# A third pass over edges whose messages are formed per step, and attribute sums moved to the second pass

## The reference, cut to what matters

```python
# L1: h = (relu(norm(x)) * deg_out ** -0.5) @ weight
rst = segment_sum(h[src], dst)
x = x + rst * deg_in ** -0.5 + bias
# L2: h = relu(norm(x))
msg = relu(h[src] + edge_attr)
agg = segment_sum(msg, dst)
x = x + relu((h + agg) @ W1 + b1) @ W2 + b2
# L3 norms [h[src], edge_attr] @ W1a over all edges, so it needs, beside others,
# segment_sum(edge_attr, dst) and edge_attr.T @ edge_attr
```

## Time and profile before

| | |
|---|---|
| median of 3 runs | 9793.06 us (9776.86 to 9793.11) |
| profiled execution | 9777.78 us, span 9775.0 us |
| busy: PE / PE weight load / DVE / ACT / POOL | 71% / 54% / 58% / 21% / 70% |
| second pass | 2966 to 5057 us |
| third pass | 5111 to 7280 us |
| granted TensorE clock in both | 0.50 of full speed (1.2 GHz) |

### The profile page before, as it was taken

The page is one execution under the profiler, slowest core; times in us unless marked ns, Lnnn a source line. Parts: engine busy times, 40 slices in busy tenths (PEclk is TensorE's granted clock), DMA queues, the critical chain, the costliest instruction groups (busy, mean ns, idle before and its releaser), DMA issues. The chain is left out here.

```text
span 9775.0 us, 180433 instructions
## 1 busy us (share of the span) xinstructions
PE 6948.1 (71%) x25668; PEld 5298.0 (54%) x25669; DVE 5675.3 (58%) x22992; ACT 2073.4 (21%) x8123; POOL 6813.4 (70%) x7038
## 2 busy tenths in 40 slices
PE   2666766675767888888845555555566888888886
PEld 1555555554556666666633333433445666666664
DVE  8777777776994444444455555555554444444444
ACT  5344444443120000000002222222211222222222
POOL 0677777776756777777757777777745777777773
PEclk8555555555555555555555555555555555555556
DMA  7333333333862222222212222222212333333334
GB/s 109 95 105 105 105 105 106 105 108 102 267 197 61 57 53 55 55 55 55 56 42 53 53 55 53 53 53 53 53 23 73 82 80 82 80 82 80 82 80 34
DMA packets 430593, 783.04 MB, mean 80 GB/s; under 512 B 179769, under 2 KB 208089, under 8 KB 429406
## 3 DMA queue, kind: packets, MB, share of 16 engines
q1 hardware_dynamic: 199054, 487.65, 17.4%
q0 software_dynamic: 216064, 278.76, 12.9%
q10 hardware_dynamic: 14544, 8.74, 0.5%
HBM read 634.79 MB, written 139.85 MB: 79 GB/s over the span
## 5 line engine op out<-in xcount | busy, mean ns | idle before, releaser
L1287 POOL DMA_INDIRECT arena<-node_table,idx x3328 | 3156.0, 948 | 1091.9 <-issue 813.1
L1225 PE MATMUL banks<-arena,onehot 128*128 x7040 | 2484.6, 472 | 1250.1 <-DVE onehot L1165 614.9
L1225 PEld LDWEIGHTS banks<-arena,onehot 128*128 128x128 f32 x7040 | 1758.8, 312 | 1871.4 <-issue 1659.9
L1408 POOL DMA_INDIRECT arena<-node_table,arena x1760 | 1660.6, 944 | 551.7 <-issue 381.8
L977 POOL DMA_INDIRECT sorted_edges<-arena,idx x1664 | 1611.2, 968 | 616.6 <-issue 576.1
L1165 DVE TENSOR_SCALAR onehot<-iota_row,block_base,edge_tables 128x128 f32<-128x128 f32 x3520 | 1255.6, 359 | 594.3 <-ACTq L1271 342.9
L922 PE MATMUL banks<-arena,onehot 128*128 x3520 | 1102.2, 424 | 568.0 <-DVE onehot L871 554.9
L922 PEld LDWEIGHTS banks<-arena,onehot 128*128 128x128 f32 x3520 | 882.5, 313 | 787.5 <-issue 780.8
L1173 DVE TENSOR_TENSOR arena<-arena,banks 128x65 f32 (+1 forms) x3520 | 895.2, 254 | 592.9 <-PE banks L1225 549.1
L1384 PE MATMUL banks<-arena 128*128 128x64 f32 x3520 | 1214.1, 448 | 0.0
L1379 PE MATMUL banks<-arena 128*64 128x65 f32 x3520 | 842.9, 343 | 392.1 <-ACT arena L1395 387.9
(11 more groups left out here) (291 smaller groups left out, 6152.7 us busy)
## 6 DMA issues: line engine op xcount, KB each, us to landing
arena<-sorted_edges SPq DMA_DIRECT2D x440, 524.0 KB, 4.5
arena<-in_attr_t SPq DMA_DIRECT2D x208, 512.0 KB
arena<-row_keys SPq DMA_DIRECT2D x110, 512.0 KB
arena<-in_attr_pairs SPq DMA_DIRECT2D x104, 512.0 KB
arena<-node_table,idx POOLq DMA_INDIRECT x3328, 2.5
arena<-node_table,arena POOLq DMA_INDIRECT x1760
sorted_edges<-arena,idx POOLq DMA_INDIRECT x1664, 2.3
sorted_edges<-blank_record SPq DMA_DIRECT2D x1, 6484.5 KB, 51.5
```

What stands on the lines that cost most here:

```text
L1225: nc.tensor.matmul(to, m.onehot[:, j % 4, :], rows, start=True, stop=True).then_inc(s["summed"], 1)
L1287: nc.gpsimd.indirect_dma_start(slot(j), None, m.table, bass.IndirectOffsetOnAxis(ap=m.idx[:, j:j + 1], axis=0)).then_inc(gathered[j % 32], 16)
L1408: nc.gpsimd.indirect_dma_start(slots[:, j % SLOTS, 0:D], None, m.table, bass.IndirectOffsetOnAxis(ap=rec_i[:, j % SLOTS, REC_DST:REC], axis=0)
```

## The change

Both passes keep their tiles, rings and plan. In the second pass SP loads the attributes into the same slots as the rows (`WIDE` = 129 columns: rows, attributes, one), so that one product and one add of 129 columns sum rows, attributes and the count; the gram leaves this pass. A tile counts as landed when its attributes are there too. In the third pass the in-place sum of tile j at step j goes. DVE forms the message of each step (all 1760) from the slots of its own tile into `m.messages`, a ring of eight, ACT applies ReLU there, and PE multiplies by 64 columns. DVE waits per group of eight steps for the tile of the last one. SP counts landed tiles between its loads. The gram is made in this pass, one product ahead of each of the 1664 steps. The pair rows are 130 apart (`STEP`) instead of 128.

```diff
+WIDE = 2 * D + 1
+STEP = 2 * RW
-EXT = 3644
+EXT = 3772
-    m.pair = m.both[:, 0:NB * 2 * D].rearrange("p (b f) -> p b f", b=NB)
+    m.pair = m.both[:, 0:NB * STEP].rearrange("p (b f) -> p b f", b=NB)
...
-    m.second_ring = arena[:, BOTH:BOTH + RING * RW]
-    m.gram_ring = [m.work[:, i * CH * D:(i + 1) * CH * D] for i in range(2)]
+    m.second_ring = arena[:, BOTH:BOTH + RING * WIDE]
+    assert RING * WIDE <= EXT + 2 * NODE
+    m.messages = tables[:, 1, 0:8 * D].rearrange("p (s f) -> p s f", f=D)
...
@@ -1088,77 +1091,89 @@
 def gather_by_tile(nc, m, a, layer):
     with ExitStack() as ctx:
-        s = sems(nc, "blank", "onehot", "summed", "added", "sum", "message", "landed", "grammed", "gram_done")
+        s = sems(nc, "blank", "onehot", "summed", "added", "sum", "message", "landed", "gram_done")
...
-        attr_in = ring(nc, "attr_in", CHUNKS if layer == 2 else 2)
+        attr_in = ring(nc, "attr_in", CHUNKS)
...
+        both_kinds = m.second_ring.rearrange("p (s f) -> p s f", f=WIDE)
+        rows, attrs = m.third_ring[:, 0, :], m.third_ring[:, 1, :]
+        width = {1: WIDE, 2: D}[layer]
         def slot(j):
-            return slots[:, j % RING * stride:j % RING * stride + D]
+            j = j % RING
+            return both_kinds[:, j, 0:D] if layer == 1 else rows[:, j * D:(j + 1) * D]
+        def load(sp, i, c):
+            t = i * RING + c * CH
+            sp.wait_ge(s["summed"], t + CH + NB - RING + SLACK)
+            settle(sp)
+            sp.dma_start(m.idx[:, c * CH:(c + 1) * CH], index[:, bass.ds(t, CH)]).then_inc(idx_in[c], 16)
+            to = both_kinds[:, c * CH:(c + 1) * CH, D:2 * D] if layer == 1 else \
+                attrs[:, c * CH * D:(c + 1) * CH * D].rearrange("p (s f) -> p s f", f=D)
+            frm = a["attr_t"][:, bass.ds(i * (RING * D) + c * (CH * D), CH * D)].rearrange("p (s f) -> p s f", f=D)
+            sp.dma_start(to, frm).then_inc(attr_in[c], 16)
+        def count(engine, i, j):
+            i, j = i + j // RING, j % RING
+            if j % CH == 0:
+                engine.wait_ge(attr_in[j // CH], i * 16 + 16)
+                if layer == 2:
+                    settle(engine)
+            engine.wait_ge(gathered[j % 32], i * (RING // 32 * 16) + j // 32 * 16 + 16)
+            if layer == 2:
+                settle(engine)
+            engine.sem_inc(s["landed"], 1)
         @block.sync
         def _(sp):
...
+            if layer == 1:
+                with sp.Fori(0, ROUNDS) as i:
+                    for c in range(CHUNKS):
+                        load(sp, i, c)
+            else:
+                def rounds(i, last):
+                    for c in range(CHUNKS):
+                        if c + 1 < CHUNKS:
+                            load(sp, i, c + 1)
+                        elif not last:
+                            load(sp, i + 1, 0)
+                        for j in range(c * CH + 8, min(c * CH + CH + 8, RING) if last else c * CH + CH + 8):
+                            count(sp, i, j)
+                sp.sem_inc(s["landed"], EARLY)
+                load(sp, 0, 0)
+                for j in range(8):
+                    count(sp, 0, j)
+                with sp.Fori(0, ROUNDS - 1) as i:
+                    rounds(i, False)
+                rounds(ROUNDS - 1, True)
         @block.vector
...
+            v.memset(m.both[:, NB * STEP:SPARE * STEP], 0.0).then_inc(s["blank"], 1)
             if layer == 1:
...
-            v.sem_inc(s["sum"], 2 * CH)
+                v.memset(both_kinds[:, :, 2 * D:WIDE], 1.0).then_inc(s["blank"], 1)
+                v.memset(m.pair[:, :, 0:D], 0.0).then_inc(s["blank"], 1)
...
-            def add_attr(i, j):
-                c = j // CH
-                dve.wait_ge(gathered[j % 32], i * (RING // 32 * 16) + j // 32 * 16 + 16)
-                if j % CH == 0:
-                    dve.wait_ge(attr_in[c], i * 16 + 16)
-                v.tensor_tensor(slot(j), slot(j), m.third_ring[:, 1, j * D:(j + 1) * D], ALU.add).then_inc(s["sum"], 1)
+            def add_attr(base, j, slots):
+                k = base + j
+                dve.wait_ge(s["summed"], ahead(k - 8, SLACK))
+                v.tensor_tensor(m.messages[:, j % 8, :], rows[:, bass.ds(slots[j] * D, D)], attrs[:, bass.ds(slots[j] * D, D)],
+                                ALU.add).then_inc(s["sum"], 1)
             def match(base, j, tiles, blocks):
                 dve.wait_ge(s["summed"], base + j - 3 + SLACK)
...
-                rows = m.both[:, bass.ds(blocks[j] * (2 * D), width)]
+                rows = m.both[:, bass.ds(blocks[j] * STEP, width)]
                 v.tensor_tensor(rows, rows, m.psum[j % 4][:, 0:width], ALU.add).then_inc(s["added"], 1)
-            def beats(base, units, i):
-                tiles, blocks = [], []
+            def beats(base, units):
+                tiles, blocks, slots = [], [], []
                 for j in range(units + 2):
                     if j < units:
                         if j % 8 == 0:
-                            if layer == 1:
-                                last = bounded_values(nc, ENG.DVE, plan[32:33, bass.ds(base + j + 7, 1)], TP - 1)[0]
+                            last = bounded_values(nc, ENG.DVE, plan[32:33, bass.ds(base + j + 7, 1)], TP - 1)[0]
                             blocks += group(nc, ENG.DVE, plan, 0, base + j, SPARE - 1)
                             tiles += group(nc, ENG.DVE, plan, 1, base + j, TP - 1)
-                            if layer == 1:
-                                dve.wait_ge(s["landed"], last + 1 + EARLY)
-                        if i is not None and layer == 2:
-                            add_attr(i, j)
+                            if layer == 2:
+                                slots += group(nc, ENG.DVE, plan, 2, base + j, RING - 1)
+                            dve.wait_ge(s["landed"], last + 1 + EARLY)
+                        if layer == 2:
+                            add_attr(base, j, slots)
                         match(base, j, tiles, blocks)
                     if j >= 2:
                         add_block(base, j - 2, blocks)
...
             with dve.Fori(0, ROUNDS) as i:
                 if layer == 1:
                     add_bias(i * SHARE)
-                beats(i * RING, RING, i)
+                beats(i * RING, RING)
             with dve.Fori(0, LAG // TAIL) as i:
-                beats(i * TAIL + TP, TAIL, None)
+                beats(i * TAIL + TP, TAIL)
         @block.tensor
         def _(pe):
-            pe.sem_inc(s["grammed"], 2)
             pe.sem_inc(s["summed"], SLACK)
             if layer == 1:
+                pe.wait_ge(s["blank"], 4)
+            else:
                 nc.tensor.matmul(m.psum[GRAM][0:D, 0:RW], m.zero[:, 0:D], m.zero[:, 0:RW], start=True, stop=False,
                                  skip_group_check=True)
-            pe.wait_ge(s["blank"], 3)
-            def step(base, j, slot_no):
+                pe.wait_ge(s["blank"], 1)
+            def step(base, j, numbers):
                 k = base + j
+                if layer == 1:
+                    if j % 8 == 0:
+                        numbers += group(nc, ENG.PE, plan, 2, k, RING - 1)
+                    frm = m.second_ring[:, bass.ds(numbers[j] * WIDE, WIDE)]
+                else:
+                    pe.wait_ge(s["message"], k + 1)
+                    frm = m.messages[:, j % 8, :]
                 pe.wait_ge(s["onehot"], ahead(k, EARLY))
                 pe.wait_ge(s["added"], ahead(k - 4, SLACK))
-                if layer == 2:
...
-            def beats(i):
+                nc.tensor.matmul(m.psum[j % 4][:, 0:width], m.onehot[:, j % 4, :], frm, start=True, stop=True
+                                 ).then_inc(s["summed"], 1)
+            def add_gram(i, j):
+                if j % CH == 0:
+                    pe.wait_ge(attr_in[j // CH], i * 16 + 16)
+                attr = attrs[:, j * D:(j + 1) * D]
+                nc.tensor.matmul(m.psum[GRAM][0:D, 0:D], attr, attr, start=False, stop=False, skip_group_check=True)
+            with pe.Fori(0, ROUNDS) as i:
+                numbers = []
                 for j in range(RING):
...
+                    if layer == 2:
+                        add_gram(i, j)
+                    step(i * RING, j, numbers)
             with pe.Fori(0, LAG // TAIL) as i:
+                numbers = []
                 for j in range(TAIL):
...
-            if layer == 1:
+                    step(i * TAIL + TP, j, numbers)
+            if layer == 2:
                 nc.tensor.matmul(m.psum[GRAM][0:D, 0:RW], m.zero[:, 0:D], m.zero[:, 0:RW], start=False, stop=True,
...
         @block.scalar
...
-            act.sem_inc(s["message"], EARLY)
-            if layer == 2:
-                a_.activation(m.pair[:, :, D:2 * D], m.zero[:, 0:D].unsqueeze(1).to_broadcast([P, NB, D]),
+            if layer == 1:
+                a_.activation(m.pair[:, :, D:WIDE], m.zero[:, 0:RW].unsqueeze(1).to_broadcast([P, NB, RW]),
```

(18 more changed lines are left out.)

54 lines of the change are left out of this document (removed).

## The result

The changed kernel takes 10017.1 us (median of 4 runs, 10014.8 to 10020.1), the kernel before 9793.1 beside it (9776.9 to 9793.4): ratio 1.023, 95% interval 1.0217 to 1.0243. The forecast was 9890 us, so the sign and the mechanism came out, and the size did not: +224 us instead of +97, outside the range.

A forecast was written before the change was run, and what follows sets the result against it. POOL paced both passes before; DVE and PE would bound the third. There 12 + 1.5 + 2150 - 3.5 + 106 = 2266 us against 2167.6, +99 with the gram's closing, rounded to +97: 9890 us, range 9812 to 9955.

The forecast's parts named there:

- Second pass: Second pass: stays at POOL's pace, 1.25 us per gather over 2080 us, so neither gain nor loss.
- Small pieces: Second pass's 256-byte attribute loads: 4.1 ns a piece, 8.3 us per chunk, 11.0 of 20.0 us with gathers; no cost.
- The bound moves to the chain of DVE and PE: Third pass: groups of 9.90 us exceed POOL's 9.45, so DVE and PE set the pace and POOL stalls on slots.
- The group: Eight third-pass steps in the rounds: 8.92 + 0.72 slots + 0.21 ReLU + 0 to 0.1 second wait, taken as 9.90 us.
- The head: Start of each third-pass group: sum, ReLU, then PE's weight load, 0.70 us against 0.49 from a match, so +0.21.
- The jump: Between third-pass rounds of 16 groups: 7.0 us beyond the groups, bounds 6.1 to 7.5.
- The last 96 steps: End of the third pass: 12 groups without the product by itself, 8.7 us each, 104 us plus 2 for jumps.
- The order of the chunks: Third pass: PE's product by itself waits for attribute chunks, so steps run at most 24 ahead of gathers; 96 steps left.
- (b): Third-pass steps follow their own tiles, ending 13 us after the last gather; needs groups under 9.0 us: 9726 us, chance 0.07.
- (a): Third pass: POOL stays the bound, groups at or under 9.5 us, old remainder not won: 9805 to 9830 us, chance 0.12.
- (d): Own-tile waits in the third pass without effect and everything else hidden: within 20 us of now, 9793, chance 0.04.
- (c): Second pass: attribute pieces bind at over 8.4 ns each; at 12.3 ns about +820, 10,700 us; chance 0.03.

The follow-up runs named there:

- e1: Changed kernel plus one unused list read per third-pass group, which the compiler dropped, so a repeat of the changed kernel: 10005.9 us.
- e11: Changed kernel with the slots list read mid-group, no separate read of the last tile number, and no gram product in the third pass (output incomplete): 9710.0 us.
- e8: Changed kernel with one more list of eight, really used, read by DVE in each third-pass group (attributes' address from a second slots list): 10135.0 us.
- e9: Changed kernel with the same four reads per third-pass group, but the next group's slots list read in the middle of a group: 9826.6 us.
- e7: Changed kernel without the separate read of the last tile number; the wait takes the eighth number of the tiles list already read: 9840.5 us.
- e10: Changed kernel with the slots list read mid-group and no separate read of the last tile number, gram still in the third pass: 9806.5 us.
- e6: Changed kernel with the gram back in the second pass and no separate read of the last tile number: 9704.9 us, ratio 0.9925 to the kernel before.
- e3_gram2: Changed kernel with the gram product moved back from the third pass to the second, everything computed: 9852.2 us.

## Why the prediction was right in its mechanism and wrong in its size

**Second pass: right.** No gain, no loss of pace: gathers 1.256 us apart where they were 1.251, and DVE waits for landed tiles (ACT's queue) in its groups. The +8 us were not foreseen. The same pass took 2083.9 us in e1 and 2088.2 in e11, so about half of it varies from execution to execution; I have no experiment for the rest.

**Small pieces: the conclusion right, the price wrong.** The second queue's packets doubled, 199,680 more, and its share went from 17.4% of 16 x 9775.0 us to 17.8% of 16 x 10015.4, that is by 1310 engine-us. The 13,312 pieces of 4096 bytes that went away cost about 0.23 us each at that queue's mean rate before (27,210 us for 487.65 MB). So the 212,992 new ones cost (1310 + 3040) / 212,992 = 20 ns each on their engine, and a chunk 2048 x 20 / 16 = 2.6 us, not 8.3. My row for small pieces was the wrong neighbour: it measured a write of one source spread over device memory, from issue to landing. Read in the second pass alone (3300 to 4900 us, before and then changed), it comes out the same:

```profile
q1 hardware_dynamic: 24480, 45.27, 9.7%
...
q1 hardware_dynamic: 185472, 44.74, 13.8%
```

13.8% of 16 x 1600 us for 84 chunks of 2048 pieces is 20.5 ns a piece, and 9.7% for 85 x 128 of 4096 bytes is 228 ns; per byte the small ones are 1.4 times as dear (index loads included in both). The doubling below 512 B that the Trainium skill ("DMA: Bandwidth & Descriptors", Specifications) led me to weigh would have been 16.6 us on my estimate; the measured 2.6 us are far from it because the base was wrong, while a loss against large pieces is there, of 1.4 times.

**The bound moves to the chain of DVE and PE: right.** POOL stalls 243 us on slots, and every round is over 160 us.

**The group: the step that failed.** Forecast 9.90, measured 10.46, 10.46, 10.80, on the average 10.57. 0.67 us too little, 208 times, is 139 us, more than the whole miss of 127. By terms:
- The gap between groups, which PE's idle time follows one to one, forecast 2.46 + 0.72 + 0.05 = 3.23, is 3.77. The slots were priced as one list more by the others' 0.6 to 0.7, and e8 confirms 0.6 for a list; but two of the four reads take 0.22 us longer than in the second pass (309 to 534 ns, and about 600 to up to 828). That is 0.45 of the 0.54 us. No row of the third pass of before could show it: its two lists take 0.60 us there.
- About every third group has 0.34 us more, +0.11 on the average. No row of before that I used shows it, and what it is stays open; it comes at fixed places of the loop's code, so it is no accident of the data.
- The head, from sum to weight load, was right: 0.72 us (6038.61 to 6039.33) for the forecast's 0.70. With the ReLU taken out only 0.15 of the 0.21 comes back.
- PE's 1.03 us per step was right (DVE's add waits for PE 0.26 us at 6034.84).

More than the size of a read, the form of the sum was at fault. I added reads to a period as if each were as dear anywhere. e9 gets 0.86 us of the group back by moving one read of 0.82. What fits before, the changed kernel, e7 and e9 alike is the sum read from PE's side: 8.09 us, and what DVE's absence with the head exceeds the 2.1 us of work in hand by.

**The jump: too dear.** Forecast 7.0 beyond the groups, measured 174.1 - 16 x 10.57 = 5.0: 13 x 2.0 = 26 us to the good. It lies under my lower bound too (6.1, whose two terms, 4.3 and 2.06, add up to 6.4). Between two rounds DVE idles 6.46 us, 2.92 more than in a group, where I had read 4.3 out of the earlier trace rows:

```profile
5658.43 0.23 DVE L1175 TENSOR_TENSOR edge_tables<-arena 128x64 f32 x1 [6.46 <-issue]
```

**The last 96 steps: too cheap.** Forecast 8.7 a group, measured 9.55; 118.5 us instead of 106. Here DVE alone sets the time: 8 x 0.71 + 3.77 = 9.45. I had priced the sums at 0.13 a step beside PE, where PE was not in the way at all. In e7, with one read less, such groups take 8.5 to 8.8.

Sum: 139 - 26 + 12 = +125 us; the third pass grew by 224.5 where I had 99, which is 125.5. (The 1.181 us a step of the second pass should read 303 / 257 = 1.179; nothing hangs on it.)

**The order of the chunks: present, tighter, and of no effect here.** The changed kernel's steps lag too far behind for it. "24 ahead" was wrong in two ways. The bound holds at a chunk's first step, 9 ahead of the landed tile, and the 15 steps behind it could get to 24 only if they took no time; at 1.1 us each they take most of the chunk's 20 us. And the chunk is only asked for when that tile is counted: its load takes 4.4 us to land, 3 to 4 gathers, and the tile's own landing 2.4 us, 2 gathers. By estimate that leaves some 4 of the 24; e10 shows 1, and the rest stays open.

**Rivals.** (b) named the right turning point: it asked for groups under 9.0 us and PE free of the chunk order, and gave 9726, 67 us under the kernel before. e6 fulfils both and runs at 9705, 73 under it. (a) and (d) were refuted by the rounds of 174 us, (c) by the pace of the second pass. The range failed since my bounds of a group, 9.6 to 10.2, moved only the terms that I had, and left no room for reads that are dearer in their new place.

## What to carry to other kernels

When an engine that feeds another one goes away to read addresses, compare its absence with the work that the other has in hand. Up to that point a read is free, beyond it each one is lost to both. Moving one read into the middle of the group was worth 179 us here, no less than deleting another (165 us). A value that is in a list already read need not be read again. And before moving a product from one pass to another, ask which of the two is nearer to its bound with it, and whether it ties the order of the steps to the order of a load.

## What was not expected of the hardware

- The same read of one number into DVE's registers took 309 ns in the second pass and 534 in the third, with hardly any spread; without that read, in e7_last, the median of the three lists rises from 607 to 815 ns, so that two of the three are slow where one was (row below). What makes them slow stays open.

```profile
L727 DVEq TENSOR_LOAD <-target_plan x561: 599/815/825, 5300.2 to 7178.5; - x187
```

- A pair of products of 129 columns takes 0.80 us where one of 65 took 0.69, and beside the product of attributes the steps are 1.13 us apart instead of 1.03 (e3_gram2). So the columns were not free, though the weight loads were the same.
- 256-byte pieces of a plain load cost 20 ns each on their engine, 1.4 times as much per byte as 4096-byte pieces, with the engines 27% busy in that pass.
- The granted clock was 0.50 in the third pass and 0.54, a mean over both levels, in the second, where PE has only half the weight loads of before (3520 against 6850, 849 us against 1362 in the earlier trace rows) and the clock was 0.50. No time hung on it: POOL paces that pass. In the pass that decides it is the lower of the two levels, 1.2 GHz, before and after.
